# Tiny loads moved into the x loads' queue, the first layer-norm coefficients moved ahead of the second chunk's moments, and the weights' replication moved to GpSimd's queue

## What is computed

```python
x = x + conv_ref(_ln_c(x), ...)          # CoDA-NO attention block with spectral convolutions
t = _to_tokens(x)
t = t + ffn_ref(_ln_t(t), W, V, gamma, beta)
```

## Time and profile before

| | |
|---|---|
| runs | 427.39 us median of 3 (427.3 to 428.25) |
| profiled execution | span 424.2 us; no time of its own is given beside the span, the median is 3.2 us above it |
| busy share | PE 82%, VectorE 80%, ScalarE 54%, GpSimd 50% |
| chain that ended last | VectorE 34%, PE 32%, GpSimd 12%, DMA 6%, issue 5%, SP's queue 4%, ScalarE 4% |
| first stage | 0 to about 62 us, spectra and scores to about 99 us |

### The profile page before, as it was taken

The page is one execution under the profiler, slowest core; times in us unless marked ns, Lnnn a source line. Parts: engine busy times, 40 slices in busy tenths (PEclk is TensorE's granted clock), DMA queues, the critical chain, the costliest instruction groups (busy, mean ns, idle before and its releaser), DMA issues.

```text
span 424.2 us, 7190 instructions
## 1 busy us (share of the span) xinstructions
PE 349.7 (82%) x2415; PEld 273.7 (65%) x2415; DVE 338.0 (80%) x995; ACT 229.5 (54%) x511; POOL 213.0 (50%) x261
## 2 busy tenths in 40 slices
PE   0289979997794899998999778878888789999950
PEld 0289965974352899987988748634454446767950
DVE  2999762766896967469999686999999759899991
ACT  0498851801023388545655125767886789899000
POOL 1389960000002699399892107887886579900000
PEclk9999999999998699999999969899999999999995
DMA  8999998999805000089799880142232500000998
GB/s 215 249 291 319 288 284 191 220 218 379 339 0 199 2 0 2 2 100 116 91 174 119 100 99 2 46 156 100 101 103 107 192 2 0 2 0 0 276 287 234
DMA packets 62999, 59.42 MB, mean 140 GB/s; under 512 B 5792, under 2 KB 55376, under 8 KB 60912
## 3 DMA queue, kind: packets, MB, share of 16 engines
q1 hardware_dynamic: 43232, 50.24, 40.0%
q0 software_dynamic: 16512, 8.39, 16.2%
q10 hardware_dynamic: 3216, 0.30, 0.7%
HBM read 38.84 MB, written 16.94 MB: 131 GB/s over the span
## 4 chain that ended last, share of the span: by engine, by line
DVE 34%; PE 32%; POOL 12%; DMA 6%; issue 5%; SPq 4%; ACT 4%; DVEq 0%; POOLq 0%; ACTq 0%
PE PS L632 30%; POOL BIG L569 8%; DVE SML L1196 6%; DVE BIG L1337 5%; DVE BIG L1529 4%; DVE BIG L1546 3%; SPq L511 3%; DMA BIG<-in_x 3%; DVE BIG L1613 3%; POOL BIG L588 2%; DMA BIG<-BIG 2%; PE PS L636 2%; DMA BIG<-xn_rows 2%; DVE BIG L1429 1%; DVE BIG L1425 1%
## 5 line engine op out<-in xcount | busy, mean ns | idle before, releaser
L632 PE MATMUL PS<-CST,BIG 128*128 128x128 f32 (+6 forms) x994 | 123.0, 312 | 13.1 <-ACT BIG L1004 4.5
L632 PEld LDWEIGHTS PS<-CST,BIG 128*128 128x128 f32 (+1 forms) x994 | 110.2, 193 | 28.8 <-DVE BIG L1529 8.3
L582 POOL COPY BIG<-BIG 128x512 f32<-128x512 f32 x24 | 29.9, 1291 | 79.2 <-DMA BIG<-xn_rows 75.3
L632 PE MATMUL PS<-BIG 128*128 128x128 f32 (+2 forms) x450 | 53.8, 368 | 5.9 <-DVE BIG L1337 5.4
L1196 DVE BATCH_NORM_STATS2 SML<-BIG 128x6 f32<-128x128 f32 x256 | 53.5, 279 | 5.8 <-DMA BIG<-in_x 4.4
L636 PEld LDWEIGHTS PS<-CST,BIG 128*128 128x128 f32 (+1 forms) x326 | 41.6, 183 | 19.5 <-issue 12.4
L632 PEld LDWEIGHTS PS<-BIG 128*128 128x128 f32 (+2 forms) x450 | 40.6, 168 | 16.7 <-issue 8.7
L636 PE MATMUL PS<-CST,BIG 128*128 128x128 f32 (+1 forms) x326 | 49.0, 291 | 2.5 <-ACT SML L400 1.4
L632 PE MATMUL PS<-BIG,SML 128*128 128x256 f32 (+4 forms) x230 | 48.8, 415 | 0.0
L400 ACT ACTIVATE BIG<-PS 128x512 f32<-128x512 f32 (+3 forms) x59 | 32.2, 569 | 26.0 <-PE PS L632 21.0
L569 POOL TENSOR_SCALAR BIG<-BIG,SML 128x128 f32<-128x128 f32 x84 | 40.3, 498 | 9.0 <-DVE SML L1216 9.0
(11 more groups left out here) (218 smaller groups left out, 487.3 us busy)
## 6 DMA issues: line engine op xcount, KB each, us to landing
xn_rows<-BIG SPq DMA_DIRECT2D x8, 1024.0 KB, 9.4
BIG<-xn_rows SPq DMA_DIRECT2D x8, 1024.0 KB, 9.2
BIG<-in_x POOLq DMA_DIRECT2D x8, 1024.0 KB, 11.0
BIG<-rs_rows SPq DMA_DIRECT2D x8, 1024.0 KB, 4.7
out_x<-BIG SPq DMA_DIRECT2D x32, 256.0 KB, 3.6
BIG<-wy_rows SPq DMA_DIRECT2D x16, 192.0 KB, 5.8
BIG<-BIG SPq DMA_DIRECT2D x16, 192.0 KB, 8.0
BIG<-in_L_conv_mixer_w SPq DMA_DIRECT2D x2, 544.0 KB, 9.1
```

The lines of the kernel that those rows point to most:

```text
L582: pool.tensor_copy(x_mix[:, g % MIX_RING], columns(g)).then_inc(S("x_mix_pool"), 1)
L632: return pe.matmul(o, l, rhs, start=start, stop=stop, **k)
```

## The change

- The 17 tiny loads leave ScalarE's queue. SP issues them, three behind each of the x chunks 2 to 6 and two behind chunk 7.
- VectorE makes the coefficients of chunk 0 before the moments of chunk 1. From there on the order is as before: moments of chunk c, then coefficients of chunk c-1.
- `LN_POOL` is now [12, 8, 12, 12, 12, 12, 8, 8] in place of [8, 8, 12, 12, 12, 12, 12, 8]. Its sum stays 84.
- The 16 loads to `wr`, with their three waits, are issued by GpSimd after its memset and no longer by SP.

```diff
-LN_POOL = [8, 8, 12, 12, 12, 12, 12, 8]
+LN_POOL = [12, 8, 12, 12, 12, 12, 8, 8]
@@ block.sync
+            small = [(name, a, k) for name, (a, k) in ROW_AT.items() if k <= NH]
             for c in range(XC):
                 tokens = slice(XR * c, XR * c + XR)
                 sp.dma_start(x_h[:, tokens, :], x_row[:, tokens, :]).then_inc(S(f"x_in{c}"), 16)
+                if c >= 2:
+                    for name, a, k in small[3 * c - 6:3 * c - 3]:
+                        sp.dma_start(PRM[:, a:a + k], flat(t[name]).to_broadcast([128, k])).then_inc(S("prm"), 16)
             sp.dma_start(CST[:, n:], t["const"][:, n:]).then_inc(S("const_in"), 16)
...
             sp.wait_ge(S("wy3"), 2)
             sp.dma_start(wy_rows, wy.rearrange("n w k h -> n (w k h)")).then_inc(S("wy_out"), 16)
-            sp.wait_ge(S("wy_out"), 16)
-            sp.wait_ge(S("rs_filled"), 48 // P1_T)
-            sp.wait_ge(S("xn_0_3"), 64)
-            for n in range(NH):
-                sp.dma_start(wr[TB * (n % HG):TB * (n % HG) + TB, n // HG].rearrange("s w k h -> s (w k h)"),
-                             wy_rows[n:n + 1, :].to_broadcast([TB, 3 * MW * MH])).then_inc(S("rep_w"), 16)
@@ block.gpsimd
             pool.memset(gf, 0.0).then_inc(S("gf_zero"), 1)
+
+            pool.wait_ge(S("wy_out"), 16)
+            pool.wait_ge(S("rs_filled"), 48 // P1_T)
+            pool.wait_ge(S("xn_0_3"), 64)
+            for n in range(NH):
+                pool.dma_start(wr[TB * (n % HG):TB * (n % HG) + TB, n // HG].rearrange("s w k h -> s (w k h)"),
+                               wy_rows[n:n + 1, :].to_broadcast([TB, 3 * MW * MH])).then_inc(S("rep_w"), 16)
@@ block.scalar
-            for name, (a, n) in ROW_AT.items():
-                if n <= NH:
-                    act.dma_start(PRM[:, a:a + n], flat(t[name]).to_broadcast([128, n])).then_inc(S("prm"), 16)
             root(ln_r[:, 0:XR], row_var[:, 0:XR], "eps_c")
@@ block.vector
-            for c in range(XC):
-                if c + 1 < XC:
-                    dve.wait_ge(S(f"x_in{c + 1}"), 16)
-                    ln_moments(c + 1, x_h, range(XR), row_var)
-                ln_coefs(c, "ln_coef")
+            ln_coefs(0, "ln_coef")
+            for c in range(1, XC):
+                dve.wait_ge(S(f"x_in{c}"), 16)
+                ln_moments(c, x_h, range(XR), row_var)
+                if c > 1:
+                    ln_coefs(c - 1, "ln_coef")
+            ln_coefs(XC - 1, "ln_coef")
```

## The result

| | median | lowest to highest | runs |
|---|---|---|---|
| kernel before | 427.82 us | 426.69 to 433.37 | 16 |
| changed kernel | 430.81 us | 427.93 to 437.74 | 16 |

The ratio is 1.0076 [1.005, 1.0101]: slower, by three quarters of a per cent. The forecast was 425.5 us, faster. The result lies on the upper edge of the range (430.8), and its sign and its mechanism are not those of the likeliest case; in size it is nearest to rival A (429.8).

A forecast was written before the change was run, and what follows sets the result against it. Bound: DMA engines' work from 66.3 us on. First `xrep` copy could land at 78.6; 10.9 us of mixed transfers plus 7.6 us end at 97.0 against 98.92, -1.9: 425.5 us. Range 423.0 to 430.8.

The forecast's parts named there:

- the likeliest case: Replication and `xrep` copies overlap on two queues; last copy lands at 97.0 against 98.92, -1.9 us, 425.5; chance 0.36.
- rival A: Replication and `xrep` copies: no overlap between queues, engines idle before 78.6; last copy at 101.3, +2.4, 429.8 us; chance 0.28.
- The true bound is the DMA engines' work from 66.3 on: Both replications, 32 DMAs of 192 KB: DMA engines limit them at 0.945 us each, 208 GB/s; SP's issue only waits.
- Tiny loads on SP. Cost 0: SP's queue between x chunks: 17 issues, 8 us, hidden behind SP's waits for room; without that cover up to 8 us.
- at 66.3 all the same: End of the first stage: `wy` lands and the weights' replication starts at 66.3, unchanged although GpSimd ends 1.8 us earlier.
- A full backlog: Last write-out, issued at 58.3, stands behind queued DMA work (share 1.03), so an earlier end gains nothing for write-outs.
- two queues at 290 GB/s: Weights' replication on GpSimd beside SP's `xrep` copies: 290 GB/s, 0.68 us per transfer, while both queues have work.
- 16 x 0.68 = 10.9: Mixed stretch of replication and `xrep` copies from 78.6: 16 transfers at 0.68 us take 10.9 us, to 89.5.
- 1.15 us per issue: GpSimd's pace for the 16 loads to `wr`, taken half-way between 0.92 and 1.39 us.
- Rival C: Weights' replication: GpSimd's descriptors held back or pace 2.26 us; products' release 107.9, 436 us, or 432 with half; chance 0.08.
- `ts` at 75.3: End of the first stage: `ts` comes 1.8 us earlier, so the first `xrep` copy is issued at 75.3, not 77.10.
- Rival D: First stage's earlier end passes on to `wy` and the weights' replication: -1.8 us more, 423.5 us; chance 0.08.

The follow-up runs named there:

- the filler: Changed kernel plus seven dummy products on TensorE behind chunk 0's groups, output unchanged; measured 1.0109 [1.0046, 1.0171] of the kernel before.
- tiny loads alone: Kernel before with only the 17 tiny loads moved to SP's queue between x's chunks; measured 1.0079 [1.003, 1.0128].
- tiny loads last: Changed kernel with all 17 tiny loads issued on SP behind x's last chunk and the second load of constants; measured 1.0136 [1.0072, 1.02] of the kernel before.
- replication back on SP: Changed kernel with the 16 loads to `wr` returned to SP's queue; measured 0.9993 [0.9953, 1.0033] of the kernel before.
- replication alone moved: Kernel before with only the 16 loads to `wr`, and their waits, moved to GpSimd; measured 1.0029 [0.9988, 1.0069].
- `wy` ahead: Kernel before with the `wy` write to DRAM issued on SP before the last normalised chunk, not behind it; measured 0.9857, then 0.995 on another chip.
- tiny loads on GpSimd: Changed kernel with the 17 tiny loads at the start of GpSimd's queue instead of SP's; measured 0.9977 [0.9916, 1.0038] of the kernel before.

## Why the prediction was wrong

**The bound was read rightly.** "The true bound is the DMA engines' work from 66.3 on": the filler shows it from one side (`ts` 1.85 us earlier than before, products no earlier for it), moving `wy` from the other (replication 3.2 us earlier, products 2.3). Its limits show too. In two profiles of the table (34.7 and 35.8 in the last column) the products waited for the scores and the softmax, with TensorE at half clock, and for no copy. And where the copies do end last, the last column is no constant, but runs from 30.9 to 34.4, and is short where the start is late: of a start later by 2.9, 5.8 and 2.2 us (tiny loads alone, tiny loads last, replication back on SP) 2.0, 4.1 and 1.4 arrive at the products. Why a third is made good is not shown.

**The step that failed first: "Tiny loads on SP. Cost 0", with `wy` landing "at 66.3 all the same".** I counted SP's issue time (8 us, hidden behind its waits for room) and that cover was real: no x chunk made VectorE late. I did not ask what the DMA engines do while SP's queue holds tiny loads. With three of them between two chunks the engines lost 0.54 MB, or 1.9 us, from 16 to 34; the backlog of the earlier trace rows did not make it good, and the replication starts 1.7 to 2.0 us later. "A full backlog" was right at 58 and was just the reason why nothing before it is free. That the tiny loads in SP's queue do it is shown by them alone (+2.9 at the replication, share 0.90), by their place in a row (+5.8, share 0.29 where they stand), and by the share of 1.05 without them; the 66.64 of that last kernel speaks less clearly, since VectorE held `wy` there. How they do it (the places in the queue) is argued.

**The second, and the larger: two queues at 290 GB/s.** With both at work they go at 224 and 225 GB/s, like one at 219. The term 16 x 0.68 = 10.9 should have been 16 x 0.945 = 15.1. The rows of 287 and 405 GB/s were of transfers to 128 partitions and said nothing on this. The Trainium skill, "DMA: Bandwidth & Descriptors", in "Issuing engines are not separate DMA queues", says that DMAs from any engine end on the same 16 DMA engines and interleave, and that a second issuer saves only sequencer time; the traces here agree (224 GB/s from 77 to 91 with the replication alone moved, 219 before). It is the rule I should have weighed. That two queues on opposite halves could double the rate was my own inference from the port swizzle, not that page's rule, and no run here shows it.

**GpSimd's cost as an issuer was mis-sized, to the other side.** 1.15 us per issue were taken, within 0.92 to 1.39; measured:

```profile
L577 POOL DMA_DIRECT2D BIG<-wy_rows x16: 489/504/732, 68.3 to 75.8; - x16
...
DMA to landing us min/median/max: 3.5/6.8/11.7
```

0.50 us each, as fast as SP's 0.54, and the quickest lands after 3.5 us, not 4.3. So rival A had the rate right, and a price near the right one (+2.4), but for a wrong reason: its idle time was to come from GpSimd's slow pace, and came from a late `wy`. What GpSimd's queue costs by itself comes from two pairs of kernels that differ in it alone: 0.6 us at the products with nothing else moved (99.57 for 99.01), and 0.0 to 1.1 with the rest of the change in (100.39, 101.43 and 101.45 for 100.38). One profile of a side does not fix it closer. Rival C is refuted: no issue took over 0.73 us, so nothing held the descriptors back. The rule of the Trainium skill that I cited for it ("SBUF — State Buffer", in "SBUF: two separate sides", on VectorE's two-port modes) had no case here, with VectorE busy for 0.27 us of 7 in the stretch from 70 to 77.

**`ts` at 75.3.** GpSimd's part came out as worked out or better (13.6 for 14.0, last token's end 56.5 to 56.8 for 58.2), but `ts` at 77.9 to 78.2. What I left out is TensorE: from 15.3 it works on chunk 0's groups, earlier than before, and then waits until 26 for the next. Its granted clock falls, and the 64 products after it take 10.06 us for 7.47. Every kernel with the early coefficients had this stretch at low clock between 24 and 35, except the one with the filler; no kernel with the old order had it. Of the 2.6 us by which the filler brings `ts` forward, 1.6 stand at the end of the first stage; 1.0 belongs to a second stretch, between 70 and 77 (granted clock 0.68), which the filler's kernel does not have. That one is not tied to the early coefficients: the replication alone moved had it too (0.69), and `wy` ahead in one profile of two. With the filler `ts` came at 75.25, the value forecast, and was worth nothing, as the bound says. So an error of 2.7 us in that step had no effect on the sum. Rival D fell with it: `wy` did not come earlier but later.

**The sum.** In the prediction's own terms, with the pace and the latency measured and 0.945 us for each transfer, the last copy lands at 66.3 + 3.5 + 31 x 0.945 = 99.1 (replication alone moved: 99.5); with the start at 68.3 that is 101.1 (changed kernel: 101.4). Of the 4.4 us between the forecast 97.0 and 101.4, 2.7 stand already in the kernel with the tiny loads on GpSimd (99.73), most of it for the rate, and 1.7 are the tiny loads. So the rate took away the forecast gain, and the tiny loads made the loss. It is +2.4, +2.4 and +1.4 us at the products in three profiles, against +1.9 [1.1, 2.6] in the pooled runs and +3.0 in the first comparison. That the size agrees with rival A's is in part luck: the rate was its reason and held, its idle time came from another cause.

**What stays open.** The three comparisons of the same kernel gave 1.0076, 0.9989 and 1.0038. From the release of the products to the end of the span the program is unchanged, yet it took 325.2 us before and 325.4 and 327.0 in the second and third profile of the changed kernel. Over all kernels the profiles differ there in where TensorE's granted clock is at half for 3.4 to 20.5 us, and how often. Whether a change in the first stage makes such stretches later on more likely was not settled: with one profile of each kernel no pattern shows. The same spread hides why `wy` ahead of the last chunk gives 3.1 us in the pooled runs [2.0, 4.1] (13 against 67 runs) and 2.3 and 0.6 at the products in its two profiles.

## What to carry to other kernels

Small transfers slipped between the large ones of a queue can leave the DMA engines partly idle even if no large one is missed where it is used; keep them on a queue that carries no large ones. ScalarE's did that before the change (share 1.07 and 1.05), GpSimd's too (1.05), though at its start they delayed its tokens by 3.1 us. Look at the share of the DMA engines before a stretch that hangs on a backlog, and send the small transfer on which the next stage waits ahead of the last large one: that one line made the best kernel here (424.7 us pooled, ratios 0.9857 and 0.995). A second queue added no rate here, where one already kept the engines busy.

## What the runs showed that I had not expected

- The tiny loads (512 bytes or 8 KB) took SP 0.43 us each, but the first one behind a chunk of 1 MB 1.5 to 3.7 us, where a chunk's own issue had taken 0.9 to 4.0.
- GpSimd issues a load of 192 KB in 0.50 us, where its 1 MB loads take 1.39 or more.
- After some 6.7 us of early work TensorE idled about 4 us, and its granted clock then was half for part of the next 8 (0.66 in the mean, 2.6 us lost). With the tiny loads moved alone the clock there stayed at 1.00, so it takes VectorE's new order and the work that it lets begin early.
